# A segment-sum and MLP kernel on one core: storing each finished group in three pieces between the edge loads

## What is computed

```
def reference(x, src, dst, edge_attr_128, W1, b1, W2, b2, W3, b3, ln_w, ln_b):
    h = max(layernorm(x), 0)                                   # x is 12500 x 128, f32
    agg = segment_sum(edge_attr_128, dst, num_segments=12500)  # edges are 200000 x 128, f32
    h = concatenate([h, agg], axis=-1)
    h = relu(h @ W1 + b1)
    h = relu(h @ W2 + b2)
    h = h @ W3 + b3
    h = (h - mean(h)) * rsqrt(var(h) + 1e-5) * ln_w + ln_b
    return x + h
```

## Time and profile before

| | |
|---|---|
| median of 3 runs | 322.18 us (321.7 to 322.6) |
| the profiled execution's own time | 321.9 us |
| its span | 320.1 us |
| PE busy | 274.8 us, 86% |
| DVE busy | 246.4 us, 77% |
| POOL busy | 178.5 us, 56% |
| ACT busy | 149.7 us, 47% |
| moved by the 16 DMA engines | 116.48 MB, mean 364 GB/s |

### The profile page before, as it was taken

One profiled execution on the slowest core, in us unless ns is written; L12 is line 12 of the kernel. 1 busy time (PEld: TensorE's weight loads), 2 busy tenths in 40 slices (PEclk: granted clock), 3 DMA queues, 4 the chain that ended last, 5 costly groups with the idle time before them and its releaser, 6 DMA issues. The chain is left out here.

```text
span 320.1 us, 12312 instructions
## 1 busy us (share of the span) xinstructions
PE 274.8 (86%) x3927; PEld 186.4 (58%) x3927; DVE 246.4 (77%) x944; ACT 149.7 (47%) x407; POOL 178.5 (56%) x208
## 2 busy tenths in 40 slices
PE   2959998998979887898888888899888888899881
PEld 0736665666646655566556666566555656566550
DVE  4944588888758887777787887778787887878785
ACT  1442555555415545545444545554444545554622
POOL 8634555566546565455565665555556565555511
PEclk9976999999979999999999999999999999999997
DMA  7999999999999999999999999999999999999992
GB/s 227 354 373 374 373 373 374 373 390 373 389 373 382 380 374 389 373 373 373 373 373 373 373 373 374 373 374 373 373 373 373 373 373 373 373 373 373 383 385 80
DMA packets 79454, 116.48 MB, mean 364 GB/s; under 512 B 3312, under 2 KB 79440, under 8 KB 79440
## 3 DMA queue, kind: packets, MB, share of 16 engines
q1 hardware_dynamic: 78426, 115.85, 102.5%
q10 hardware_dynamic: 1014, 0.46, 0.5%
HBM read 109.90 MB, written 6.40 MB: 363 GB/s over the span
## 5 line engine op out<-in xcount | busy, mean ns | idle before, releaser
L777 POOL TENSOR_SCALAR place<-iota,rows_at 128x128 f32<-128x128 f32 x131 | 104.5, 801 | 107.1 <-PE place_ps L426 98.4
L415 PE MATMUL part_ps<-ring,onehot 128*32 128x128 f32 x3120 | 115.1, 282 | 25.9 <-DMA ring<-in_edge_attr 24.9
L415 PEld LDWEIGHTS part_ps<-ring,onehot 128*32 128x32 f32 x3120 | 79.4, 111 | 72.4 <-issue 51.9
L931 DVE TENSOR_TENSOR agg<-place_ps,agg 128x128 f32 x131 | 38.0, 290 | 53.7 <-PE place_ps L426 51.9
L426 PE MATMUL place_ps<-place,part 128*128 128x128 f32 (+1 forms) x262 | 64.9, 330 | 2.7 <-POOL place L777 2.3
L785 POOL TENSOR_TENSOR xs<-xs,vecs 128x384 f32 (+2 forms) x33 | 54.8, 1659 | 19.0 <-ACT h L646 19.0
L855 DVE TENSOR_TENSOR onehot<-iota,local_t 128x768 f32<-128x768 f32 x66 | 63.5, 964 | 0.3 <-issue 0.3
L632 ACT ACTIVATE part<-part_ps 128x128 f32<-128x128 f32 x131 | 34.9, 267 | 48.5 <-PE part_ps L415 46.8
L426 PEld LDWEIGHTS place_ps<-place,part 128*128 128x128 f32 (+1 forms) x262 | 40.0, 192 | 30.0 <-issue 22.6
L646 ACT ACTIVATE h<-xs,x_shift,x_rstd 128x128 f32 (+2 forms) x98 | 41.3, 483 | 2.4 <-DVE x_shift L848 2.4
L662 ACT ACTIVATE hid<-hid_ps,b1s 128x384 f32<-128x384 f32 (+1 forms) x33 | 19.0, 576 | 47.5 <-PE hid_ps L450 47.5
(11 more groups left out here) (86 smaller groups left out, 202.0 us busy)
## 6 DMA issues: line engine op xcount, KB each, us to landing
ring<-in_edge_attr SPq DMA_DIRECT2D x130, 768.0 KB, 11.6
xs<-in_x SPq DMA_DIRECT2D x32, 192.0 KB, 10.1
out_x<-xs SPq DMA_DIRECT2D x15, 384.0 KB
dst_i<-in_dst SPq DMA_DIRECT2D x1, 768.0 KB
ring<-in_edge_attr SPq DMA_DIRECT2D x1, 192.0 KB, 10.1
out_x<-xs SPq DMA_DIRECT2D x1, 192.0 KB
out_x<-xs ACTq DMA_DIRECT2D x1, 192.0 KB
xs<-in_x SPq DMA_DIRECT2D x1, 96.0 KB
```

The costliest lines, as they stand in the source:

```text
L415: last = nc.tensor.matmul(part_ps[par_q % 2][s * WIN:(s + 1) * WIN, 0:D], onehot[:, oct_par, first + s, j, :], e[:, s, j * D:(j + 1) * D], ...
L777: nc.gpsimd.tensor_scalar(place[:, par_q % 2, :], iota[:, 0:P], rows_at[:, k:k + 1], None, ALU.is_equal).then_inc(place_ready, 1)
L931: nc.vector.tensor_tensor(v, place_ps[par_q % 2][:, 0:P], v, ALU.add).then_inc(added, 1)
```

## The change

`STORED_EARLY` and the loop that goes with it are gone. Step `i` of SP now stores group `i - 3` (`BEHIND = 3`) in three pieces: the partitions 0 to 47 after its first reload, 48 to 95 after its second, and 96 to 127 after its third (`OUT_PARTS`). The first piece waits for `out_ready`. The steps 0, 1 and 2, written out, store nothing; the steps 3 to 28 store the groups 0 to 25. Behind the load of the tail rows stay two `store_two`, for the groups 26 to 29; what follows is as before.

```
-STORED_EARLY = 8
+BEHIND = 3
+OUT_PARTS = ((0, 48), (48, 96), (96, P))
...
+                def store_part(g, k):
+
+                    p0, p1 = OUT_PARTS[k]
+                    if k == 0:
+                        sp.wait_ge(out_ready, g + 1)
+                    rows = out[bass.ds(g * CHUNK + p0 * PER, (p1 - p0) * PER), :]
+                    sp.dma_start(rows.rearrange("(p j) f -> p (j f)", j=PER),
+                                 xs[p0:p1, bass.ds(g * CHUNK, CHUNK)]).then_inc(stored, 16)
+
...
-                    def step(i, par, pairs):
+                    def step(i, par, pairs, storing=True):
 
                         load_x(i + XAHEAD, (par + XAHEAD) % 2, pairs + (par + XAHEAD) // 2)
                         for k in range(4):
                             reload(4 * i + RING + AHEAD + k, (4 * par + AHEAD + k) % RING)
-
-                    step(0, 0, 0)
-                    with sp.Fori(0, STORED_EARLY // 2) as t:
-                        step(2 * t + 1, 1, t)
-                        step(2 * t + 2, 0, t + 1)
-                        store_two(2 * t)
-                    with sp.Fori(STORED_EARLY // 2, (STEPS - 3) // 2) as t:
+                            if storing and k < len(OUT_PARTS):
+                                store_part(i - BEHIND, k)
+
+                    step(0, 0, 0, storing=False)
+                    step(1, 1, 0, storing=False)
+                    step(2, 0, 1, storing=False)
+                    with sp.Fori(1, (STEPS - 3) // 2) as t:
                         step(2 * t + 1, 1, t)
                         step(2 * t + 2, 0, t + 1)
                     sp.wait_ge(seg_done, QUADS - RING + 1)
...
-                    for g in range(STORED_EARLY, GROUPS - 2, 2):
+                    kept = STEPS - 2 - BEHIND
+                    for g in range(kept, GROUPS - 2, 2):
                         store_two(g)
                     store(GROUPS - 2)
                     store_last(GROUPS)
-                    sp.wait_ge(stored, 16 * ((GROUPS - 2) // 2 + 2 + len(LAST_PARTS)))
+                    sp.wait_ge(stored, 16 * (len(OUT_PARTS) * kept + (GROUPS - 2 - kept) // 2 + 2 + len(LAST_PARTS)))
```

## The result

| | before | after |
|---|---|---|
| median | 321.64 us (20 runs) | 322.51 us (20 runs) |
| after over before | | 1.0032, 95% interval 1.0016 to 1.0047 |
| profiled execution, span | 320.1 us | 321.2 us |

The change makes the kernel slower by 0.3%, 1.0 us (0.5 to 1.5 by the interval). The forecast was 1.1 us faster. The first view of the changed kernel is its page: span, DMA and GB/s in 40 slices, and its rows of transfers with their median time to landing.

What follows compares the result with a forecast made beforehand. Transfers set the pace, the DMA engines being full. Removing the early pairs gives -2.8 us, the pieces +1.8, together -1.1 with the first term unrounded: 321.9 to 320.8 us, range 319.1 to 324.8.

Steps and rivals of the forecast that it cites:

- The bulk: Eleven pair stores behind the last loads, draining beside the end's chain of small steps; claimed to cost nothing, removal gaining nothing.
- The price of the pairs: Four early pair stores among the loads: 0.71 us each, so removing them brings the last quads 2.8 us sooner.
- rival D: Queues: the cost of a transfer by itself decides, +1.3 us on the forecast, 322.1 us; chance 0.08.
- The two levels: DMA rate limits: all loads together at most 373 GB/s, everything at most about 397 or 398, so one engine's store is free.
- the term of 0.07 us a group: Steps: cost of a group's pieces where neighbouring pieces overlap, taken as smooth; 25 x 0.07 = 1.8 us.
- raised stretch: Us after an early pair's issue in which the rate rises, for the first pair from 64 to 69 us, to 399 GB/s.
- 0.11 by whole engines: Steps: the same overlap cost if each instant counts none, one or two engines on a store; 0.11 us a step.
- rival B: Every step's first three reloads: engines reach pieces in clusters, 0.22 us a group, +2.7 us, 324.6 us; chance 0.22.
- Rival A: Steps: stores ride wholly free beside the loads, 395 GB/s, 319.1 us; chance 0.15.
- C: Steps: the pairs' price holds for any store, 0.353 us a group, +6.0 us, 327.9 us, 380 GB/s; chance 0.06.
- the chain of 12.05 us: End: small steps from the last quad's sum at 305.02 to the last issue at 317.07; claimed to stay 12.05 us.

Runs made afterwards that it cites:

- three adjacent pieces: Changed kernel with the three pieces of a group all issued behind the step's first reload, one directly behind another; 384 GB/s in the steps, execution 324.76 us.
- the double store: Changed kernel with four pieces a step, each stored twice, to the output and to an unread scratch tensor in HBM; 397 GB/s, costing 0.45 us a step.
- one third alone: Changed kernel storing only the first piece of each step, partitions 0 to 47; 378 GB/s, the piece costing 0.08 us.
- the one with four early groups: Changed kernel with groups 0 to 3 in four pieces each in steps 3 to 6, the others in thirteen pairs behind the last load; 0.9950 of the kernel before.
- the three fastest versions: Versions storing no groups, eight in fours or four in fours in the steps, the others behind the last load; 0.9958, 0.9945 and 0.9950 of the kernel before.

## Why the prediction was wrong

**What held.** Transfers set the pace. The bulk was hidden. SP was not the bound (its issues of quads fell to a median of 0.37 us while those of the pieces held it for 1.1 to 1.7 us) and never waited for an output in the steps. The price of the pairs, 2.8 us, stands by the rates of the earlier trace rows, and by landings too: from the 21st quad to the 65th it takes 101.3 us in the kernel before and 98.5 without stores. A transfer by itself shows no cost, as three adjacent pieces against one tell, so rival D falls. The two levels, 373 for loads and 397 for everything, were right; the double store showed the second directly.

The Trainium skill ("DMA: Bandwidth & Descriptors", Anatomy of one DMA — SWDGE (gpsimd) path) gives a fixed part of about 2 us for each transfer, fitted to transfers issued by GpSimd, and 65 more of them would be an estimated 130 us. In full queues of SP's transfers the runs show none of it: the change cost 1.0 us in all.

**The step that failed** is the term of 0.07 us a group, "I take 0.07, since nothing below a us shows in the raised stretch". Measured: 0.19 by the rate, 0.15 or 0.16 by the landings of the quads. The working spread the engines' visits to a piece evenly over 4.0 us and counted their mean. The run with one third alone shows that they are not even: a store is in flight for 1.9 us, not 2.96, and eight of the 16 engines finish the piece within 0.7 us, five only 2.5 us or more after the first. The raised stretch of a pair could not show it, because an engine's visit to a pair, 0.99 us, bridges the gaps between them, 0.8 us at most; a visit of 0.185 us doesn't. The row that I read had the wrong length for what I asked of it. The term is 25 x 0.12 = 3.0 us too small by the rate, 2.0 to 2.3 by the landings. The other value in the working, 0.11 by whole engines, was too small as well, for the same reason.

This is rival B by mechanism and nearly by price: 0.22 a group was forecast, 386 GB/s in the slices; 0.19 and 387 were measured. "Against: the pieces are a third as long" had it the wrong way round. Rival A is out (it needed 395), C too (380).

**The second error** had the other sign: the chain of 12.05 us was taken as fixed. It was 10.88 and 10.87 in the changed kernel, 1.2 us less. Together: loads 1.8 to 2.0 us later by the rates (1.5 to 1.8 by the landings) less 1.2 us is 0.6 to 0.8 us (0.3 to 0.6), against 1.0 measured with an interval of 0.5 to 1.5. The sum lies at the low end of the interval; what may be left over is not attributed. Without the shorter chain the change would have cost about 2 us. Had only the second been missed, the sum would have been 2.3 us faster. That the forecast missed by 2 us and not by 3 is luck: two errors of opposite sign.

**What stays open.** Why the register loads at the end are slow in the kernel before, in the one with four early groups and in the double store, and not in the others, and whether they make the chain long or only go with it. A bulk beside them doesn't decide it. Neither the layout of the code nor the moment of the load was tried. Nor do the runs show why the engines lie apart in clusters, or what holds loads alone below 397.

## What to carry to other kernels

When transfers fill the queues, work moved in among them is free only as far as the transfers there leave a rate unused (here 373 of 397 GB/s); measure that opening with a store as short as the one you mean to insert, since a long one hides the gaps between engines. A store that drains behind the last load under other work is already free, so the question for each group is not how cheaply it travels in the steps but whether the end still has room for it: the three fastest versions here stored at most eight groups in the steps. And a chain at the end that "moves rigidly" should be compared in a second kernel before its length is carried over.

## What the runs showed of the hardware

The rate with all queues full has two levels here: 373 GB/s when only 1,536-byte rows are loaded, 397 when stores are always among them or alone. The kernels with less in their steps lie between the levels. The packet records of the traces show the same from below: in the same window a packet of 1,536 bytes takes 69 ns in the median with loads alone and 65 ns with the double store. The 16 engines don't work in step: the increments for one store are 3.1 us apart from first to last with one third alone, 3.4 to 3.5 for the pairs of the kernel before, and up to 4.8 with one piece a step. The depth of the backlog changed with the mixture: a quad lands 11.6 or 11.7 us after its issue (medians) with five transfers a step, 11.2 or 11.3 with six, 9.4 or 9.5 with nine and 8.7 with thirteen; with eight it was 9.6 when they were spread and 10.4 when three were adjacent. And a register load from SBUF that takes 0.34 us in the loops took 0.75 to 1.94 us in the written-out end, in every kernel.
